# A fused decoder layer: routed weights of the experts spread by DMA, routing and small DVE steps in other rounds

## The chip, the cores and the metric

One core of a Trainium2 chip runs the whole layer as one program. The metric is the device time of one execution in microseconds (us), lower is better. The engines are PE (matrix products), ACT, DVE and POOL (elementwise work), and SP, whose queue issues most of the DMAs. They run side by side, each in its own program order, and wait for each other by semaphores.

## The reference

```python
x = x + local_attention(layernorm(x))              # 8 heads, chunks of 12 with 12 past, relative positions
x = x + cross_attention(layernorm(x), ctx_1024)    # 16 heads of 64, 512 context rows, rotary keys, clipped scores
x = x + ffn(layernorm(x))
def ffn(x):                                        # 1024 tokens of 128
    x_addr = x @ P_w.T
    dw1, dw2, dw3 = (route(x_addr @ U.T) for U in (U1, U2, U3))  # top 3 of 12, softmax over them, else 0
    h = gelu(sum_e (x @ W1[e].T) * dw1[:, e])      # 128 -> 512, 12 experts
    return sum_e (h @ W2[e].T) * dw2[:, e] + dw3 @ b2
```

Four batch entries of 256 tokens; all in fp32.

## The kernel before

The program has three stages. The local attention takes about the first 60 us. The cross attention follows in 32 **rounds** (`for r in range(NPAIR)`), each for a pair of heads of one batch entry (8 rounds per entry): PE makes the scores of the next pair (L1211), the values of a coming group (`unit`, L1027 to L1029), the rotated keys of a coming pair (`key_products`, L1016 to L1018, up to round 25), in even rounds the queries of the next four heads (`queries`, L1145 to L1147), then the weighted values (`weigh_values`, L1230) and the sums of the weights (`sum_weights`, L1240). ACT exponentiates, DVE clips (L1631), turns keys (`key_unit`, L1512 and L1517) and divides (`divide`: a reciprocal, L1638, and a product into `o_t`, L1642). POOL adds up the weights (L578, `halves_summed` L584) and adds the swapped key halves (L570). PE's `queries(j)` waits until `divide` has read the bank that it writes, `divide` of round r - 1 being DVE's first step in round r. DVE's round r starts when PE has made the sums of round r - 1.

Small steps are set into the rounds by tables. `LATENT_ROUNDS[b]` gives, for batch entry b, the rounds in which DVE takes the statistics of its tokens, normalizes them and takes statistics again, and normalizes again (`latents`, parts 0, 1, 2; L1457, L1451). `extras` gives the rounds after which PE turns those tokens or projects a batch entry's output (`project`, 16 products for two halves of 8, L1249; its sum into the tokens on DVE is L1650 or L1653). `context_lo` (L1503), `latents_lo` (L1602) and `output_bias` (L1597, in rounds 6 and 26) are further DVE steps. The **routing** of the first 512 tokens runs in seven stages two half rounds apart from `NORM_ROUND` = 22 on: weights, tokens, address, scores (r = 25), chosen (26), softmax (27), turn (28).

The third stage is the mixture of experts. `first_mixture(n)` runs for n = 0 to 23: two halves of 512 tokens by 12 experts, each 12 products of 128x512 (L1374 to L1376, four banks of three). Before it the tokens are multiplied by their routed weight (`expert_tokens` on DVE, L1681, or `pool_tokens` on POOL, L647), and split into `xeT_hi` (ACT, L853) and `xeT_lo` (POOL, L607). DVE also turns and splits an expert's weights for each n (`turn_weights` L1661, `weights_lo` L1667). The routed weights of a half, `dw`, are turned on PE (L1301) and copied by ACT to `gate_src`; SP stores them to DRAM and loads them back spread over all 128 partitions, three experts to a load (`store_gates` L474, `load_gates` L487, two buffers in `gates`). For the first three experts of each half, e < `GE`, no load is made: PE spreads their weights by a product with a selection matrix (`spread_weights`, L1278, six in all) from `dw1T`, which ACT and DVE make in two steps (L876, L1712) before ACT copies `gate_src`. SP's queue takes the gate loads in order between its loads of expert weights (`GATE_AT`), which each wait until a ring slot is free.

The last sums (`sum_weights(31)`) are issued after expert 0, the last projection (32 products, two token tiles) after expert 1; then come DVE's additions to x (L1817), the statistics of the second half's tokens and its routing (`ROUTE_2`: tokens in expert 5, address and scores in 6, chosen 7, softmax 8, turn 9). After expert 11 ACT applies the Gelu (L957) to the banks that expert 12 writes next. The second mixture follows from about 354 us on.

## Time and profile before

| | |
|---|---|
| time, median of 3 runs | 425.8 us (425.7 to 427.06) |
| the profiled execution: its time, its span | 426.81 us, 424.9 us |
| PE busy | 402.7 us, 95% of the span, 3040 instructions |
| DVE busy | 336.0 us, 79%, 655 |
| POOL busy | 257.5 us, 61%, 225 |
| ACT busy | 178.2 us, 42%, 282 |
| mean granted TensorE clock | 0.996 |

PE is busy nearly throughout, but its products are pipelined and their ends are modelled, so a short wait can hide in a busy stretch. Busy shares are means over stages of different limits: DVE is busy 19.9 of 20 us in some stretches of the rounds and half of the time in the second mixture. What an edit is worth is read from the wait that ends last at its place: the entries in brackets at a PE instruction, and the engine named there.

### The profile page before, as it was taken

The numbers are of one execution on the slowest core, as the hardware profiler recorded it, in microseconds if no ns is written. First come the engines' busy times: TensorE is split into PE (matmuls) and PEld (weight loads), VectorE is DVE, ScalarE is ACT, GpSimd is POOL, SyncE is SP. The second block draws the span as 40 slices with busy tenths as digits, with TensorE's granted clock in tenths as the row PEclk, the third lists the DMA queues.
The fourth block names the chain that finished last, engine by engine and source line by source line (L and its number), as shares of the span: only waits on it lengthen the run. The fifth ranks groups of instructions, "written<-read, shape, count | busy, mean of one in ns | idle before, by whom it ended". The sixth has DMA issues, their size and how long they took to land.

```text
span 424.9 us, 8269 instructions
## 1 busy us (share of the span) xinstructions
PE 402.7 (95%) x3040; PEld 296.0 (70%) x3040; DVE 336.0 (79%) x655; ACT 178.2 (42%) x282; POOL 257.5 (61%) x225
## 2 busy tenths in 40 slices
PE   3988799999999999999999998999999999999996
PEld 2666686667657776677766675687767788888884
DVE  8887759999989988998877997885778772655554
ACT  6867354545445245544263534336256443000000
POOL 6823549999998977998987686758335840000000
PEclk9999989999999999999999999999999999999999
DMA  7687422221211112111111162547347640000000
GB/s 181 160 214 105 89 66 61 52 81 44 51 44 32 38 37 52 26 45 43 40 37 39 41 110 65 137 69 153 54 107 155 148 64 2 6 13 8 6 6 14
DMA packets 84746, 28.63 MB, mean 67 GB/s; under 512 B 71957, under 2 KB 79050, under 8 KB 84706
## 3 DMA queue, kind: packets, MB, share of 16 engines
q1 hardware_dynamic: 81748, 26.80, 28.6%
q10 hardware_dynamic: 2958, 1.30, 1.4%
q8 instruction: 25, 0.41, 0.4%
q14 instruction: 15, 0.12, 0.1%
HBM read 17.67 MB, written 2.02 MB: 46 GB/s over the span
## 4 chain that ended last, share of the span: by engine, by line
PE 58%; DVE 31%; issue 4%; ACT 2%; DMA 2%; ACTq 1%; POOL 0%; DVEq 0%
PE psum L1230 7%; DVE rden L1638 7%; PE psum L1211 6%; DVE e_sb L1631 6%; PE psum L1414 5%; PE psum L1415 5%; PE psum L1413 5%; PE psum L1374 4%; PE psum L1376 4%; PE psum L1375 4%; PE psum L1249 3%; PE psum L1240 2%; DVE rope_b L1512 2%; DVE xn L1457 2%; DVE kT L1517 2%
## 5 line engine op out<-in xcount | busy, mean ns | idle before, releaser
L578 POOL TENSOR_TENSOR e_part<-e_sb 128x512 f32<-128x512 f32 x64 | 88.4, 1397 | 25.7 <-DVE e_sb L1631 25.7
L839 ACT ACTIVATE e_sb<-psum 128x1024 f32<-128x1024 f32 x64 | 62.3, 1023 | 81.4 <-PE psum L1211 78.5
L1631 DVE TENSOR_SCALAR e_sb<-e_sb 128x1024 f32<-128x1024 f32 x64 | 63.8, 1026 | 5.9 <-ACT e_sb L839 5.9
L1211 PE MATMUL psum<-q_t,kT 64*128 64x256 f32 x512 | 64.2, 389 | 0.0
L1230 PE MATMUL psum<-e_sb,v_sb 128*64 128x256 f32 x512 | 63.8, 386 | 0.0
L1638 DVE RECIPROCAL rden<-psum 128x256 f32<-128x256 f32 x32 | 55.9, 1747 | 9.1 <-PE psum L1240 9.1
L1840 DVE SCALAR_TENSOR_TENSOR x_sb<-psum,dw,x_sb 128x128 f32<-128x128 f32 x96 | 33.7, 351 | 37.1 <-PE psum L1415 34.5
L1211 PEld LDWEIGHTS psum<-q_t,kT 64*128 64x128 f32 x512 | 46.7, 186 | 13.9 <-issue 8.4
L1230 PEld LDWEIGHTS psum<-e_sb,v_sb 128*64 128x64 f32 x512 | 33.7, 136 | 22.3 <-issue 6.6
L607 POOL TENSOR_TENSOR xeT_lo<-xeT,xeT_hi 128x512 fp32r<-128x512 f32 x24 | 31.4, 1309 | 28.7 <-ACT xeT_hi L853 28.6
L570 POOL TENSOR_TENSOR kT<-kT,raw 128x512 f32<-128x512 f32 x32 | 44.2, 1382 | 2.7 <-DMA raw<-rope_b 1.9
L584 POOL TENSOR_TENSOR e_part<-e_part 128x512 f32<-128x512 f32 x32 | 42.1, 1317 | 2.5
L1374 PE MATMUL psum<-xeT_hi,w1T_hi 128*128 128x512 f32 x96 | 38.9, 406 | 0.8 <-ACT h_f L957 0.5
L1414 PE MATMUL psum<-w2T_lo,h_hi 128*128 128x512 f32 x96 | 38.0, 396 | 0.0
L1415 PE MATMUL psum<-w2T_hi,h_lo 128*128 128x512 f32 x96 | 37.8, 394 | 0.0
L1376 PE MATMUL psum<-xeT_hi,w1T_lo 128*128 128x512 f32 x96 | 37.5, 390 | 0.0
L1375 PE MATMUL psum<-xeT_lo,w1T_hi 128*128 128x512 f32 x96 | 37.4, 390 | 0.0
L1413 PE MATMUL psum<-w2T_hi,h_hi 128*128 128x512 f32 x96 | 37.3, 389 | 0.0
L853 ACT ACTIVATE xeT_hi<-xeT 128x512 fp32r<-128x512 f32 x24 | 15.2, 632 | 27.5 <-DVE xeT L1681 21.9
L1374 PEld LDWEIGHTS psum<-xeT_hi,w1T_hi 128*128 128x128 f32 x96 | 18.0, 188 | 7.0 <-issue 2.6
L1517 DVE TENSOR_TENSOR kT<-psum,cosT 128x512 f32<-128x512 f32 x32 | 21.7, 677 | 0.0
L1661 DVE STREAM_TRANSPOSE psum<-w_raw 128x512 f32<-128x512 f32 x24 | 17.4, 726 | 4.8 <-DMA w_raw<-in_L_ffn_W_dram 2.8
(202 smaller groups left out, 733.3 us busy)
## 6 DMA issues: line engine op xcount, KB each, us to landing
raw<-rope_b SPq DMA_DIRECT2D x116, 64.0 KB, 2.0
w_raw<-in_L_ffn_W_dram SPq DMA_DIRECT2D x96, 64.0 KB, 2.3
gates<-gate_dram SPq DMA_DIRECT2D x6, 768.0 KB, 5.0
ctx_sb<-in_ctx_dram SPq DMA_DIRECT2D x4, 256.0 KB, 6.7
vbd<-v_dram SPq DMA_DIRECT2D x16, 52.6 KB
v_dram<-v_tok SPq DMA_DIRECT2D x4, 136.0 KB
raw<-in_L_xattn_Wkv_dram SPq DMA_DIRECT2D x2, 256.0 KB, 5.5
kT<-in_L_xattn_Wkv_dram SPq DMA_DIRECT2D x2, 256.0 KB, 4.8
```

The costliest lines, as they stand in the source:

```text
L578: pool.tensor_tensor(e_part[:, p % 2, half, :, :], e_sb[:, i % ERING, :, 0, :], e_sb[:, i % ERING, :, 1, :], ALU.add)\
L839: act.activation(e_sb[:, i % ERING, :, :, :].rearrange("p a k t -> p (a k t)"), psum[:, a:a + 2, :].rearrange("p a b -> p (a b)"), ACT.Exp ...
L1211: mm = pe.matmul(psum[:, 2 * (i % 2) + a, t * S:(t + 1) * S], key_slot(p)[rows, kt * P:(kt + 1) * P], q_t[rows, j % 2, p % 2, :], start=Tr ...
L1230: mm = pe.matmul(psum[DX * a:DX * a + DX, pv_bank(p), 0:S], v_sb[g % 2][:, kt, 2 * pp + a, :], e_sb[:, i % ERING, a, t, :], start=(kt == 0 ...
L1374: pe.matmul(bank(c), w1T_hi[:, e, c, :], hi, start=(e == 0), stop=False)
L1375: pe.matmul(bank(c), w1T_hi[:, e, c, :], lo, start=False, stop=False)
L1376: mm = pe.matmul(bank(c), w1T_lo[:, e, c, :], hi, start=False, stop=(e == NE - 1))
L1413: pe.matmul(o, hi, w_hi, start=(c == 0), stop=False)
L1414: pe.matmul(o, hi, w_lo, start=False, stop=False)
L1415: mm = pe.matmul(o, lo, w_hi, start=False, stop=(c == HC - 1))
L1631: dve.tensor_scalar(e, e, E_LO, E_HI, ALU.max, ALU.min).then_inc(s["clip_done"], 1)
L1638: dve.reciprocal(rden[:, p % 2, :], psum[:, pv_bank(p), S:2 * S]).then_inc(s["rden_done"], 1)
```

## The change

All routed weights now come by DMA. `spread_weights`, `pick`, `spread` and `dw1T` are gone, with ACT's and DVE's two steps for `dw1T`. `GLOADS` has eight loads instead of six; the first (experts 0 to 2 of the first half) lands in a part of `w1T_hi` that is filled with expert weights only later. `expert_tokens` and `pool_tokens` read all gates from SBUF. The routing of the first half starts at round 20 instead of 22, that of the second half one expert earlier. The last sums are issued after half of expert 0, the last projection after half of expert 1; DVE's additions and statistics that follow stand one expert earlier. The steps for the latents, the context rests, the output bias and two projections stand in other rounds; the first statistics of an entry's latents are apart from the rest. The diff, cut (tables first, then SP, ACT, PE and DVE):

```diff
-    GLOADS = [(half, q) for half in range(2) for q in range(1, NE // GE)]
-    GATE_AT = {4: (0, 1), 10: (2,), 14: (3,), 16: (4,), 20: (5,)}
+    GLOADS = [(half, q) for half in range(2) for q in range(NE // GE)]
+    GATE_AT = {4: (0, 1, 2), 10: (3,), 13: (4,), 15: (5,), 19: (6,), 22: (7,)}
+    GATE_HOME = 6
...
-        LATENT_ROUNDS = {1: (0, 1, 2), 2: (9, 10, 11), 3: (14, 15, 16)}
+        LATENT_ROUNDS = {1: (1, 2, 3), 2: (5, 6, 10), 3: (11, 13, 16)}
+        LATENT_TURN = {4: 1, 12: 2, 18: 3}
+        CONTEXT_REST = {8: 2, 17: 3}
...
-        extras = {rounds[2] + 1: ("latents", b) for b, rounds in LATENT_ROUNDS.items()}
+        extras = {r: ("latents", b) for r, b in LATENT_TURN.items()}
...
-                extras[b * PPB + 3 + 2 * t] = ("project", b - 1, t)
+                extras[b * PPB + (1 if b == 2 else 3) + 2 * t] = ("project", b - 1, t)
...
+        def gate_tile(g, j):
+            if g:
+                return gates[:, (g - 1) % 2, j, :]
+            return w1T_hi[:, GATE_HOME + j, :, :].bitcast(F32).rearrange("p c q -> p (c q)")
...
-        NORM_ROUND = (B - 1) * PPB - 2
+        NORM_ROUND = (B - 1) * PPB - 4
-        ROUTE_2 = {"tokens": 5, "address": 6, "scores": 6, "chosen": 7, "softmax": 8, "turn": 9}
+        ROUTE_2 = {"tokens": 4, "address": 5, "scores": 5, "chosen": 6, "softmax": 7, "turn": 8}
...
                 if g == 0:
+                    sp.wait_ge(s["unit_ps"], len(UNIT))
+                    sp.wait_ge(s["misc_ps"], MISC_NO["keys", NPAIR - 1] + 1)
+                elif g == 1:
                     sp.wait_ge(s["pv_ps"], STEPS - HG)
                     sp.wait_ge(s["round_q_ps"], NQ - 1)
...
-                    act.activation(dw1T[0:NE, :], bank(at, NE), ACT.Copy).then_inc(s["dw1_hi_done"], 1)
-                    act.wait_ge(s["dw1_lo_done"], half + 1)
...
-                if r in (NPAIR - 3, NPAIR - 2):
-                    spread_weights(r - NPAIR + 3)
...
+                        if EXTRA_NO[what]:
+                            pe.wait_ge(s["extra_read"], EXTRA_NO[what])
...
-                    if c == 1 and beside == "spread":
-                        spread_weights(NE)
+                    if c == 1 and beside == "sums":
+                        sum_weights(NPAIR - 1)
+                    elif c == 1 and beside == "project":
+                        for t in range(TPB):
+                            last = project(B - 1, t, psum[:, 7, t * D:(t + 1) * D])
+                        last.then_inc(s["tail_ps"], 1)
...
-                first_mixture(n, "spread" if n + 2 == NE else ROUTE_MID.get(n))
-                if n == 0:
-                    sum_weights(NPAIR - 1)
-                if n == 1:
-                    for t in range(TPB):
-                        mm = project(B - 1, t, psum[:, 7, t * D:(t + 1) * D])
-                    mm.then_inc(s["tail_ps"], 1)
+                first_mixture(n, ("sums", "project")[n] if n < 2 else ROUTE_MID.get(n))
...
-                if e < GE:
-                    dve.wait_ge(s["spread_ps"], half * GE + e + 1)
-                    gate = bank(gate_bank(n))
-                else:
-                    gate = gates[:, g % 2, e % GE, :]
-                dve.tensor_tensor(xeT[:, n % 2, :], gate, xnT[:, half, :], ALU.mult).then_inc(s["xe_done"], 1)
+                dve.tensor_tensor(xeT[:, n % 2, :], gate_tile(g, e % GE), xnT[:, half, :], ALU.mult).then_inc(s["xe_done"], 1)
...
-            beside = {6: (output_bias, 0), NPAIR - 6: (output_bias, 1)}
+            beside = {4: (output_bias, 0), NPAIR - 6: (output_bias, 1)}
...
-                if r - 1 in CONTEXT_ROUND:
-                    context_lo(CONTEXT_ROUND[r - 1])
+                if r in CONTEXT_REST:
+                    context_lo(CONTEXT_REST[r])
...
-                if n == 4:
+                if n == 2:
                     final_norm(1, 1)
-                if n == 2:
+                if n == 1:
                     dve.wait_ge(s["tail_ps"], 1)
```

## Rows read from the trace of the kernel before

**Rows 1.** Windows: us, then busy us of PE, PEld, DVE, ACT, POOL, clock, DMA
```profile
100.00:120.00 20.00, 19.09 (x142) 13.27 (x140) 19.90 (x23) 9.86 (x14) 18.29 (x13) 1.00 0.17 43
345.00:385.00 40.00, 40.00 (x175) 32.65 (x174) 19.92 (x49) 5.97 (x11) 2.20 (x2) 1.00 0.05 10
```
**Rows 2.** Lines grouped, PE: count, busy us, mean ns, idle before
```profile
L1278 PE MATMUL psum<-dw1T,spread 44*128 44x512 f32 x6 | 3.1, 520 | 0.8 <-DVE xeT L1681 0.8
```
**Rows 3.** PE's waits in the rounds: one grouped row (total, times, longest), three from the timeline
```profile
PE psum L1145 <- DVE o_t L1642: 3.6, 5, 1.3
...
118.34 0.35 PE L1145 MATMUL psum<-lat_hi,wq_hi 128*128 128x256 f32 x1 [0.91 <-DVE o_t L1642]
144.36 0.50 PE L1016 MATMUL psum<-wkv_hi,ctx_hi 128*128 128x512 f32 x1 [0.67 <-DVE x_sb L1650]
256.43 0.35 PE L1145 MATMUL psum<-lat_hi,wq_hi 128*128 128x256 f32 x1 [1.26 <-DVE o_t L1642]
```
**Rows 4.** DVE timeline, rounds 1 to 8: start us, busy us
```profile
69.53 1.74 DVE L1638 RECIPROCAL rden<-psum 128x256 f32<-128x256 f32 x1
71.64 1.57 DVE L1457 TENSOR_SCALAR xn<-x_sb,mv,rstd 128x128 f32<-128x128 f32 x2
73.93 1.57 DVE L1631 TENSOR_SCALAR e_sb<-e_sb 128x1024 f32<-128x1024 f32 x2
...
114.28 1.79 DVE L1503 TENSOR_TENSOR ctx_lo<-ctx_f,ctx_hi 128x512 fp32r<-128x512 f32 x1
115.99 1.75 DVE L1638 RECIPROCAL rden<-psum 128x256 f32<-128x256 f32 x1
```
**Rows 5.** Timeline of DVE at rounds 25 and 28, and of PE after round 27
```profile
232.90 1.76 DVE L1638 RECIPROCAL rden<-psum 128x256 f32<-128x256 f32 x1 [1.47 <-PE psum L1240]
254.08 1.75 DVE L1638 RECIPROCAL rden<-psum 128x256 f32<-128x256 f32 x1
...
251.19 2.05 PE L1249 MATMUL psum<-wo_sb,o_t 128*128 128x128 f32 x16
```
**Rows 6.** PE timeline, from round 29 to the last projection
```profile
264.76 2.05 PE L1249 MATMUL psum<-wo_sb,o_t 128*128 128x128 f32 x16
273.81 0.47 PE L1278 MATMUL psum<-dw1T,spread 44*128 44x512 f32 x1 [0.76 <-DVE xeT L1681]
280.61 3.73 PE L1249 MATMUL psum<-wo_sb,o_t 128*128 128x128 f32 x32
```
**Rows 7.** DVE timeline, from round 29 to the last division; POOL's last sum of weights
```profile
266.85 0.29 DVE L1653 TENSOR_TENSOR x_sb<-psum,x_sb 128x128 f32<-128x128 f32 x1 [1.72 <-PE psum L1249]
279.65 0.42 DVE L1642 TENSOR_TENSOR o_t<-psum,rden 128x256 f32<-128x256 f32 x1
...
274.10 1.29 POOL L584 TENSOR_TENSOR e_part<-e_part 128x512 f32<-128x512 f32 x1
```
**Rows 8.** The tile gates: DVE's products (ns min/median/max), and the loads' time to landing
```profile
L1681 DVE TENSOR_TENSOR xeT<-gates,xnT x10: 658/684/1301, 280.0 to 345.2; 128x512 f32<-128x512 f32 x10
...
DMA to landing us min/median/max: 4.2/5.0/5.8
```
**Rows 9.** SP's queue in the timeline: expert weights 0 to 3, the second half's gates
```profile
244.25 9.44 SPq L509 DMA_DIRECT2D w_raw<-in_L_ffn_W_dram  x16
...
311.88 0.33 SPq L474 DMA_DIRECT2D gate_dram<-gate_src  x1
313.42 0.35 SPq L487 DMA_DIRECT2D gates<-gate_dram  x1
```
**Rows 10.** Second half: scores, turn, and expert 12's start on PE; first gated tokens on DVE
```profile
298.23 1.08 PE L1296 MATMUL psum<-uT,addrT 64*128 64x36 f32 x8
308.54 0.60 PE L1301 MATMUL psum<-ident,dw 128*12 128x128 f32 x4 [0.24 <-DVE dw L1735]
318.19 0.47 PE L1374 MATMUL psum<-xeT_hi,w1T_hi 128*128 128x512 f32 x1 [0.50 <-ACT h_f L957]
...
313.80 1.33 DVE L1681 TENSOR_TENSOR xeT<-psum,xnT 128x512 f32<-128x512 f32 x2
```

More of the change, by code:

```diff
@@ L247, in decoder_layer @@
         uT = sb("uT", [DADDR, NR * NE], F32, third)
-        pick = sb("pick", [SPLIT, NE], F32, third)
-        spread = sb("spread", [SPLIT, GE, P], F32R, third)
         gate_src = sb("gate_src", [NE, 4 * P], F32, third)
@@ L261, in decoder_layer @@
         dw = sb("dw", [P, 2, 4, NR, NE], F32, third)
-        dw1T = sb("dw1T", [SPLIT, 4 * P], F32R, third)
         h_lo = sb("h_lo", [P, 2, HC, 4 * P], F32R, third)
@@ L354, in swap_halves, with gate_sem, gate_landed @@
                      .then_inc(s[f"swapped{p % 2}"], 16)
-        def gate_bank(n):
-            return 5 if n < 2 else 5 - n % 2
+        def gate_tile(g, j):
+            if g:
+                return gates[:, (g - 1) % 2, j, :]
+            return w1T_hi[:, GATE_HOME + j, :, :].bitcast(F32).rearrange("p c q -> p (c q)")
+        def gate_sem(g):
+            return s["ld_gate2" if g == 0 else f"ld_gate{(g - 1) % 2}"]
+        def gate_landed(queue, g):
+            queue.wait_ge(gate_sem(g), 16 if g == 0 else 16 * ((g - 1) // 2 + 1))
         def pv_bank(p):
@@ L366, in queries_bank @@
             return pv_bank(2 * j - 1) if j else MISC_BANK
-        NORM_ROUND = (B - 1) * PPB - 2
+        NORM_ROUND = (B - 1) * PPB - 4
         ROUTE = {"weights": 2 * NORM_ROUND, "tokens": 2 * NORM_ROUND + 2, "address": 2 * NORM_ROUND + 4, "scores": 2 * NORM_ROUND + 6,
                  "chosen": 2 * NORM_ROUND + 8, "softmax": 2 * NORM_ROUND + 10, "turn": 2 * NORM_ROUND + 12}
-        ROUTE_READ = {"weights": ("rt_done", 2), "tokens": ("fT_done", 1), "address": ("addr_done", 1), "scores": ("z_done", 1)}
-        FILLED = 20
-        ROUTE_2 = {"tokens": 5, "address": 6, "scores": 6, "chosen": 7, "softmax": 8, "turn": 9}
-        ROUTE_MID = {5: "tokens", 6: "scores", 9: "turn"}
+        ROUTE_READ = {"weights": ("rt_done", 2), "tokens": ("fT_done", 1), "address": ("addr_done", 1), "scores": ("z_done", 1), "turn": ("gate_src_done", 1)}
+        FILLED = 18
+        ROUTE_2 = {"tokens": 4, "address": 5, "scores": 5, "chosen": 6, "softmax": 7, "turn": 8}
+        ROUTE_MID = {4: "tokens", 5: "scores", 8: "turn"}
         POOL_TOKENS = tuple(range(4, NE, 2)) + tuple(range(NE + 4, 2 * NE, 2))
@@ L486, in load_gates @@
                 rows = gate_dram[half, q * GE:(q + 1) * GE].rearrange("e t -> (e t)")
-                sp.dma_start(gates[:, g % 2, :, :].rearrange("p e t -> p (e t)"), rows.partition_broadcast(P)).then_inc(s[f"ld_gate{g % 2}"], 16)
+                if g:
+                    to = gates[:, (g - 1) % 2, :, :].rearrange("p e t -> p (e t)")
+                else:
+                    to = w1T_hi[:, GATE_HOME:GATE_HOME + GE, :, :].bitcast(F32).rearrange("p e c q -> p (e c q)")
+                sp.dma_start(to, rows.partition_broadcast(P)).then_inc(gate_sem(g), 16)
             for p in range(5, 8):
@@ L645, in pool_tokens @@
                 pool.wait_ge(s["xeT_lo_done"], n - 1)
-                pool.wait_ge(s[f"ld_gate{g % 2}"], 16 * (g // 2 + 1))
-                pool.tensor_tensor(xeT[:, n % 2, :], gates[:, g % 2, e % GE, :], xnT[:, half, :], ALU.mult).then_inc(s["xe_pool_done"], 1)
+                gate_landed(pool, g)
+                pool.tensor_tensor(xeT[:, n % 2, :], gate_tile(g, e % GE), xnT[:, half, :], ALU.mult).then_inc(s["xe_pool_done"], 1)
             for n in range(1, 2 * NE):
                 token_rest(n)
-                if n == 4:
+                if n == 3:
                     rstd_of(LN_F + NT // 2, NT // 2)
@@ L873, in route @@
                     act.wait_ge(s["dw1_ps"], half + 1)
-                    if half == 0:
-                        act.wait_ge(s["fill_done"], 3)
-                    act.activation(dw1T[0:NE, :], bank(at, NE), ACT.Copy).then_inc(s["dw1_hi_done"], 1)
-                    act.wait_ge(s["dw1_lo_done"], half + 1)
                     if half:
@@ L943, in _ @@
                     tokens_hi(n + 2)
-                if n == 4:
+                if n == 3:
                     final_normalize(1)
@@ L1418, in _ @@
             for n in range(2 * NE):
-                if n < 2 * NE - 2 and n + 2 != NE:
-                    spread_weights(n + 2)
                 if n in BIAS:
@@ L1709, in route @@
                     return
-                if stage == "turn":
-                    dve.wait_ge(s["dw1_hi_done"], half + 1)
-                    dve.tensor_tensor(dw1T[REST:SPLIT, :], bank(at, NE), dw1T[0:NE, :].bitcast(F32), ALU.subtract)\
-                       .then_inc(s["dw1_lo_done"], 1)
                 if stage not in ("chosen", "softmax"):
```

31 lines of the change are left out of this document (6 added, 25 removed).

## The prediction

> **What bounds the kernel now.** I read the page first (PE busy for 95% of the span), then the windows, then PE's timeline for the waits in brackets, then the timeline of whichever engine a bracket names. The windows show that the page's share hides two stages [rows 1]. From 345 us on PE has no idle time at all, 175 products in 40.0 us, 0.229 us each, with DVE half idle: there only work taken from PE counts, and the change takes none there. In the rounds, at 100 to 120 us, PE is busy for 19.1 of 20 us but DVE for 19.9: PE and DVE are level, and where DVE's round runs over, PE waits. Its waits are short: five of them before the queries, 3.6 us in all, and one of 0.67 before a value product, all on DVE [rows 3]. The third stage to read is the passage from the rounds into the experts, 260 to 320 us, where each few microseconds have another engine that comes last.
>
> The sum is made against the profiled execution, 426.81 us with a span of 424.9 (1.9 lie around it), and carried over to the median of 425.8, which lies 1.0 below that execution.
>
> **The six spread products** cost 0.52 each on PE, 3.1 us in all, with a wait of 0.76 before the third [rows 2, 6]. That is the price if PE were the last engine wherever one stood. It isn't, so each place is taken by itself below.
>
> **Latents, context rests, bias (rounds 0 to 19).** DVE runs from its division at 69.53 (round 1) to the one at 115.99 (round 8) without a wait, and PE's queries of round 8 then wait 0.91 for that division [rows 3, 4]. So what is added to DVE in rounds 1 to 7 moves PE's round 8. A normalization with its statistics takes 71.64 to 73.93 = 2.3 us, 0.7 of it statistics; a context rest 114.28 to 115.99 = 1.7 [rows 4]. Into rounds 1 to 7 come the first statistics of entry 1 (from round 0, 0.7), those of entry 2 (0.7) and its first normalization (2.3); out goes one context rest (1.7). The bias and the low half of the latents only change rounds within. That is +2.0 us for DVE. The 0.7 from round 0 frees DVE there, so +1.3 at PE's round 8. Rounds 9 to 16 lose the same steps, and the wait of 0.67 at 144.36 can go with the share of the other three query waits (3.6 less 0.91 and 1.26: 1.4) that lies there, put at a third, 0.5: 1.2 regained [rows 3]. I take +0.1. The ends: +2.0 if nothing is regained, and -3.0 if every wait but round 28's goes (3.6 less 1.26, plus 0.67). The wait that is added for PE before an extra step asks for readers of a round or more ago, and behind it stand only the next round's scores: nothing. Moving two projections from rounds 19 and 21 to 17 and 19 costs PE the same products.
>
> **Routing of the first half, two rounds earlier.** Today rounds 25 to 27 (scores, chosen, softmax) hold DVE from 232.90 to 254.08, 21.2 us; PE has made those rounds by 251.19, 18.3 us after the sums that released DVE at 232.90 [rows 5]. PE's queries of round 28 pay 1.26 for it, after a projection of 2.0 has covered part [rows 3, 5]. In rounds 23 to 25 DVE has two more key turns, two 128x512 products each at about 0.68 as the tokens' [rows 8], 1.3 each, and loses the bias of round 26 (1.7, as the context rest): 21.2 + 2.6 - 1.7 = 22.1. PE has two more sets of three key products, 0.7 each: 19.7. DVE is then 2.4 late instead of 2.9, but before round 26's queries stands a value unit of 0.7 as cover where the projection of 2.0 stood: wait 1.26 - 0.5 + 1.3 = 2.1 in place of 1.26, +0.8. The other end is -1.3, no wait at all. The chosen and softmax steps stand between POOL's additions and may run faster or slower than in the old rounds, so I take +0.2. The weights' transpose, token and address products are PE's in any round: nothing.
>
> **The gates of the first experts** come by DMA without cost as I read it. SP is busy with expert weights until 244.25 + 9.44 = 253.7; store to load takes 313.42 - 311.88 = 1.5, the landing up to 5.8: 261.0 [rows 8, 9]. DVE multiplies the first tokens right after its addition at 266.85 [rows 7]. The cover is 5 us. Were it gone, each microsecond would go onto DVE's chain below. The two loads behind it wait for round 28's queries as today's two do, and the next weight load for DVE's first transpose, so SP's queue keeps its order.
>
> **Round 29 to expert 2.** DVE waits 1.72 for the projection that PE starts at 264.76, adds it at 266.85, and from there runs without a wait to the end of the last division, 279.65 + 0.42 = 280.07 [rows 6, 7]: tokens and weights of experts 0 to 2 are in that chain, and none of it goes. The spread of round 29 stands before that projection, so the chain starts 0.5 earlier. The spread of round 30 and the one at 273.81 with its 0.76 stand beside the chain: PE only arrives earlier at what it waits for. The last sums amid expert 0 wait for POOL's addition (274.10 + 1.29 = 275.4 today, 274.9 then), with half of expert 0 queued behind; PE passes expert 1's first half at 274.9 + 0.5 + 12 x 0.229 = 278.2. The last projection needs the division: 280.07 - 0.5 = 279.55. Behind it, and this is new, stand six products of expert 1, 1.4 us. Today the projection starts at 280.61 with nothing of expert 1 left. So expert 2 starts at 279.55 + p + 1.4 against 280.61 + p, p being the projection itself: **+0.35**. Here the spreads' removal is used up.
>
> To this comes c, what the tokens of experts 0 to 2 cost more when their gate lies in SBUF. Ten such products take 0.684 in the median, as from PSUM (0.68, two in 1.33), but one took 1.30 [rows 8, 10]. I take c = 0 by the median; the other end is three slow ones, 1.9. The Trainium skill (SBUF — State Buffer, Who interferes with whom) speaks against this edit: a DVE instruction with two SBUF inputs contends with a GpSimd instruction that reads SBUF, and the one that comes second waits for the whole of the other. The one slow product agrees, and by that rule c would be above 0 here.
>
> **Experts 2 to 12.** The second half's scores stand at 298.23, the turn at 308.54 after a wait of 0.24 for DVE, 10.3 later [rows 10]. The scores come one expert (12 x 0.229 = 2.75) earlier against expert 2 (today 284.1, 280.61 + 3.5), so the turn at 284.1 + 14.1 - 2.75 + 10.3 = 305.75 in today's frame. From the turn to the store it is 3.3 us today, through ACT, DVE and ACT [rows 9, 10]; with only one ACT copy left about 0.5 + 0.9 = 1.4: 307.15. The load follows 1.5 later, and lands 4.2 to 5.8 after: 312.85 to 314.45, 313.65 with the median [rows 8, 9]. From the first gated tokens at 313.80 to expert 12 it takes 4.39, since ACT must split the tokens of 12 and 13 before it loads the Gelu's table and frees the banks [rows 10]. So expert 12 starts at 313.65 + 4.39 = 318.05 against 318.19: -0.15, from -0.95 to +0.65. The three spreads of this stretch (1.6 us of PE) vanish in that wait. DVE stands before the missing gates in the meantime, and behind it weights that the second mixture needs much later.
>
> **Sum:** +0.1 + 0.2 + 0.35 - 0.15 = +0.5, so 427.3 for the profiled execution and 426.3 for the median: within what can't be told from no change. A measurement of this kernel tells about 0.3% (1.3 us).
>
> **Rivals.** (1) *DVE's rounds don't lengthen.* The moved steps fall where DVE stands behind POOL today; then the waits of 0.91, 0.67 and 1.26 go and nothing replaces them: -2.85 + 0.35 - 0.15 = -2.65, 423.2. For it speaks that the statistics read one tensor and that a DVE round with nothing extra is well under PE's; against it the 46 us of DVE without a wait [rows 4]. (2) *The products have their full price*: PE is the last engine wherever a spread stood, so 3.1 + 0.76 go, 421.9. DVE's unbroken chain [rows 7] speaks against it. (3) *Port contention*: POOL adds weights all through 266 to 275 us, so all three tokens of c are slow; +0.5 + 1.9 = 428.2. It decides from c = 0.8 on. The skill's rule above would have it so wherever POOL starts first. (4) *Gates late*: the second half's load lands at 5.8 us with weight loads around it; expert 12 then starts 0.65 late instead of 0.15 early, and with the upper end of the routing (+0.8) it gives +0.5 + 0.8 + 0.6 = 427.7. That the DMA replaces the product without a gain is the forecast itself.
>
> **How the numbers follow.** Forecast 0.40; rival 1 0.24 and rival 2 0.08, so faster by over 0.3% 0.32; rival 3 0.18 and rival 4 0.10, so slower 0.28. The likeliest case alone has 425.1 to 427.0. Both signs hold much of the chance, so the range takes in rivals 1, 3 and 4 and the ends of the terms around them: 422.6 to 428.5; rival 2 and the ends of the first term lie outside.
>
> **What would show it.** In the trace after: PE's wait before the queries of rounds 4, 6 or 8 in place of round 2, and of round 26 in place of 28; a PE wait before the last projection of about 1.4 us, on the division; a wait of some tenths before the last sums, on POOL; L1681's first three at 0.68 or at 1.3; gates that land 4 to 6 us after their issue, and expert 12 within 1 us of them plus 4.4. The prediction is wrong if DVE shows idle time in rounds 3 to 7, if the last projection starts right behind expert 1's first half, or if expert 12 starts on the end of expert 11 alone.

## The result, and the profile after

| | before | after |
|---|---|---|
| median | 425.93 us (425.7 to 427.06, 4 runs) | 432.81 us (429.53 to 436.15, 4 runs) |
| ratio to before | | 1.012, 95% interval 1.0073 to 1.0166 |
| the profiled execution: time, span | 426.81, 424.9 us | 429.53, 427.6 us |

The change makes the kernel slower, where the forecast was no measurable change, 426.3 us in a range of 422.6 to 428.5. The profiled execution of after is its shortest, so there are two things to explain: the 2.7 us between the two profiled executions, and the 3.3 us from there to after's median. One of after's four runs, 436.15, counts as slow and is in its median but not in the ratio: without it the median is 431.91.

The page of after, first part (busy us and share of the span):

```profile
PE 400.4 (94%) x3034; PEld 293.9 (69%) x3034; DVE 339.3 (79%) x653; ACT 177.0 (41%) x280; POOL 256.0 (60%) x222
```

The six products are gone, and PE is busy 2.3 us less than before in a longer span: it waits 27.2 us in place of 22.2. The timeline of after's PE, its waits in brackets and the points at which I cut the span (L1153 are the queries, L1248 the sums of weights, L1257 the last projection, L1367 experts 12 and 16, L1410 and L1412 the second mixture):

```profile
67.06 0.60 PE L1248 MATMUL psum<-e_part,ones 128*64 128x256 f32 x4
...
90.93 0.35 PE L1153 MATMUL psum<-lat_hi,wq_hi 128*128 128x256 f32 x1 [1.24 <-DVE o_t L1631]
104.95 0.35 PE L1153 MATMUL psum<-lat_hi,wq_hi 128*128 128x256 f32 x1 [1.05 <-DVE o_t L1631]
131.05 0.36 PE L1153 MATMUL psum<-lat_hi,wq_hi 128*128 128x256 f32 x1 [0.69 <-DVE o_t L1631]
243.00 0.35 PE L1153 MATMUL psum<-lat_hi,wq_hi 128*128 128x256 f32 x1 [1.06 <-DVE o_t L1631]
...
269.06 0.60 PE L1248 MATMUL psum<-e_part,ones 128*64 128x256 f32 x4
275.24 0.65 PE L1248 MATMUL psum<-e_part,ones 128*64 128x256 f32 x4 [1.11 <-POOL e_part L599]
280.64 3.81 PE L1257 MATMUL psum<-wo_sb,o_t 128*128 128x128 f32 x32 [1.29 <-DVE o_t L1631]
308.15 0.60 PE L1294 MATMUL psum<-ident,dw 128*12 128x128 f32 x4 [1.67 <-DVE dw L1715]
319.51 0.47 PE L1367 MATMUL psum<-xeT_hi,w1T_hi 128*128 128x512 f32 x1 [1.21 <-ACT h_f L965]
336.11 0.50 PE L1367 MATMUL psum<-xeT_hi,w1T_hi 128*128 128x512 f32 x1 [0.51 <-POOL xeT_lo L622]
356.61 0.39 PE L1410 MATMUL psum<-w2T_hi,h_hi 128*128 128x512 f32 x1
...
423.57 0.40 PE L1412 MATMUL psum<-w2T_hi,h_lo 128*128 128x512 f32 x1
```

From starts such as these, each profile falls into five stretches: (a) sums of the first round to sums of round 30, (b) on to the last projection, (c) on to expert 12, (d) on to the second mixture, (e) its first to its last product. They are the table by which all kernels are compared below.

| kernel | median us (runs) | ratio to before, interval | a | b | c | d | e |
|---|---|---|---|---|---|---|---|
| before | | | 202.53 | 9.94 | 37.58 | 36.31 | 66.33 |
| after | 432.81 (4) | 1.012, 1.0073–1.0166 | 202.00 | 11.58 | 38.87 | 37.10 | 66.96 |
| x1 after again | 434.37 (4) | 1.0155, 1.0095–1.0216 | 204.89 | 11.57 | 39.05 | 38.09 | 66.96 |
| x2 late loads earlier | 430.37 (7) | 1.0092, 1.0058–1.0125 | 202.82 | 11.59 | 39.11 | 36.31 | 66.96 |
| x3 sums, projection not amid | 429.64 (10) | 1.0082, 1.0053–1.0111 | 202.09 | 11.61 | 38.65 | 37.06 | 66.97 |
| x4 rounds only | 426.72 (10) | 1.0008, 0.9981–1.0034 | 202.84 | 9.95 | 37.58 | 36.31 | 66.33 |
| x5 = x2 + x3 | 430.55 (4) | 1.0104, 1.0068–1.0141 | 202.72 | 11.60 | 38.34 | 36.31 | 66.96 |
| x6 first half by products | 430.60 (4) | 1.0119, 1.0070–1.0169 | 203.06 | 9.37 | 39.07 | 38.09 | 66.33 |
| x7 second half by products | 429.37 (4) | 1.0078, 1.0055–1.0101 | 202.57 | 11.58 | 39.69 | 36.30 | 66.32 |
| x8 = x5 + x6 | 428.34 (10) | 1.0044, 1.0024–1.0064 | 205.92 | 9.93 | 38.42 | 36.31 | 66.33 |
| x9 padded | 431.01 (4) | 1.0109, 1.0060–1.0158 | 202.85 | 11.57 | 39.10 | 36.96 | 66.33 |
| x10 softmax first | 430.43 (6) | 1.0102, 1.0070–1.0134 | 201.86 | 11.60 | 39.16 | 37.12 | 66.97 |
| x11 x4, softmax first | 425.66 (12) | 0.9983, 0.9963–1.0003 | 202.88 | 9.94 | 37.58 | 36.32 | 66.32 |
| x12 x4, softmax amid | 430.15 (6) | 1.0086, 1.0056–1.0116 | 204.93 | 9.92 | 37.58 | 36.28 | 66.33 |
| x13 x11, first half by DMA | 427.66 (12) | 1.0019, 1.0004–1.0034 | 201.43 | 11.63 | 37.68 | 36.29 | 66.33 |
| x14 x11, second half by DMA | 427.46 (12) | 1.0025, 1.0004–1.0045 | 202.66 | 9.94 | 38.30 | 36.31 | 66.33 |
| x15 x11 again | 426.50 (12) | 0.9997, 0.9978–1.0016 | 202.11 | 9.92 | 37.57 | 36.31 | 66.33 |

After against before: a -0.53, b +1.64, c +1.29, d +0.79, e +0.63, together +3.82. The spans differ by only 2.7 because the profiled execution of before lost 1.1 ahead of stretch a. That is chance: over the 17 profiles stretch a starts between 66.88 us (x12) and 69.75 (x9), where no edit is aimed. Stretch a itself spreads too, by its first four rounds above all: x11 and x15 are the same kernel and have 202.88 and 202.11. So a difference of less than about 0.8 in a says nothing. b and e repeat to some hundredths in the same code; among after, x1, x9 and x10, whose instructions there are the same, c spreads by 0.3 and d by 1.1.

The windows ahead of stretch a (clock is the 1.00 or 0.52 near the end of a row), of before:

```profile
52.60:56.10 3.50, 3.50 (x39) 2.92 (x41) 1.60 (x7) 1.92 (x5) 1.61 (x2) 0.52 0.38 94
```

and of after:

```profile
52.60:56.10 3.50, 3.09 (x77) 2.40 (x77) 1.90 (x8) 1.82 (x4) 1.45 (x2) 1.00 0.38 96
```

In before, PE did 39 products there at about the half level of its clock (1.2 GHz), where after did 77 at the full one (2.4 GHz). In six other profiles (x5, x8, x9, x11, x14, x15) the clock of 50 to 70 us is below 1.00 too, in kernels of both kinds.

### The profile page after: what moved, and what is told of

Read it like the earlier page. It is cut to its first block, busy times and chain, and to the rows that moved or that the text cites. A ratio compares the mean times of both kernels' runs of the same rounds, so it can differ in the third digit from the quotient of the medians.

```text
span 427.6 us, 8251 instructions
## 1 busy us (share of the span) xinstructions
PE 400.4 (94%) x3034; PEld 293.9 (69%) x3034; DVE 339.3 (79%) x653; ACT 177.0 (41%) x280; POOL 256.0 (60%) x222
## 4 chain that ended last, share of the span: by engine, by line
PE 54%; DVE 30%; issue 5%; SPq 4%; ACT 3%; DMA 2%; ACTq 1%; POOL 1%; DVEq 0%; POOLq 0%
PE psum L1238 7%; DVE rden L1627 7%; PE psum L1219 7%; DVE e_sb L1620 5%; PE psum L1411 5%; PE psum L1412 5%; PE psum L1410 5%; SPq L524 4%; PE psum L1257 3%; PE psum L1367 3%; PE psum L1369 2%; PE psum L1368 2%; DVE rope_b L1501 2%; DVE kT L1506 2%; DVE xn L1446 2%
## 5 line engine op out<-in xcount | busy, mean ns | idle before, releaser
L1367 PE MATMUL psum<-xeT_hi,w1T_hi 128*128 128x512 f32 x96 | 38.7, 403 | 2.0 <-ACT h_f L965 1.2
L1412 PE MATMUL psum<-w2T_hi,h_lo 128*128 128x512 f32 x96 | 37.9, 395 | 0.0
L1410 PE MATMUL psum<-w2T_hi,h_hi 128*128 128x512 f32 x96 | 37.7, 393 | 0.0
L1367 PEld LDWEIGHTS psum<-xeT_hi,w1T_hi 128*128 128x128 f32 x96 | 18.0, 188 | 8.3 <-POOL xeT_lo L622 2.4
L544 POOL TENSOR_SCALAR veps<-mv 128x4 f32<-128x4 f32 (+1 forms) x16 | 9.2, 572 | 21.8 <-DVE mv L1443 21.8
```

The costliest lines, as they stand in the source:

```text
L1367: pe.matmul(bank(c), w1T_hi[:, e, c, :], hi, start=(e == 0), stop=False)
L1410: pe.matmul(o, hi, w_hi, start=(c == 0), stop=False)
L1412: mm = pe.matmul(o, lo, w_hi, start=False, stop=(c == HC - 1))
```

## The experiments

Each ratio is to runs of before on the same chip.

**x1: the changed kernel once more.** No edit.

> The changed kernel itself, once more. Theory A (the tail: gate products from SBUF that wait for POOL, gate loads 6 and 7 that land too late; on top of it PE's clock, which falls in some executions after PE's new waits): fastest execution near 429.5, others up to 436, their mean granted clock 0.99 to 0.996, and where a profile catches it a stretch at half clock after one of PE's waits between 270 and 320 us. Rival B (the spread of the times has nothing to do with the clock, say the gate loads' landing): slow executions at a clock of 1.0 as well.

434.37 us: the loss is real. Its profile, 435.51 us, is 6.0 longer than the first one of the same program, in three places: a is 2.89 longer, d 0.99, and a starts 2.0 later. Most of the last is a wait for a load in the local attention, which after's first profile does not have:

```profile
48.07 2.52 PE L1103 MATMUL psum<-vbd,prT 96*32 96x68 f32 x128 [1.54 <-DMA vbd<-v_dram]
```

Stretch a parts in round 25. The timeline of after there: the first product of the softmax on DVE, POOL's two additions of weights that run beside it, and PE's weighted values behind its wait (1.06, above):

```profile
239.14 0.30 DVE L1709 TENSOR_TENSOR chosen<-chosen,ez 128x144 f32<-128x144 f32 x1
...
237.50 3.06 POOL L593 TENSOR_TENSOR e_part<-e_sb 128x512 f32<-128x512 f32 x2 [1.66 <-DVE e_sb L1620]
...
243.88 1.08 PE L1238 MATMUL psum<-e_sb,v_sb 128*64 128x256 f32 x8
```

The same in x1:

```profile
241.33 1.41 DVE L1709 TENSOR_TENSOR chosen<-chosen,ez 128x144 f32<-128x144 f32 x1
...
239.69 2.89 POOL L593 TENSOR_TENSOR e_part<-e_sb 128x512 f32<-128x512 f32 x2 [1.66 <-DVE e_sb L1620]
...
246.38 0.36 PE L1153 MATMUL psum<-lat_hi,wq_hi 128*128 128x256 f32 x1 [2.25 <-DVE o_t L1631]
247.73 1.98 PE L1238 MATMUL psum<-e_sb,v_sb 128*64 128x256 f32 x8
```

This is a race. One addition takes 1.27, so in x1 the second of the pair begins about 239.69 + 2.89 - 1.27 = 241.31, and DVE's product at 241.33: it takes 1.41 instead of 0.30 and ends when POOL is through, so it came second. In after the second addition begins at 239.12 or 239.13, against 239.14 for DVE; here the product is short and POOL's pair took 3.06 instead of 2.89, so DVE came first. The starts alone do not tell who won: the product's stands 0.01 to 0.02 behind the addition's in all ten profiles with this order (after, x1 to x9). It was lost in two of them, x1 and x8. The lost race makes PE wait 2.25 before round 26's queries instead of 1.06. Then its eight products take 1.98 instead of 1.08, with the granted clock at the half level. From the sums of round 25 to those of round 26 it is 10.54 us in x1 and x8, and 7.79 to 7.84 in the eight others: a lost race costs 2.7, and the rest of the 2.89 is a's spread. The window 240 to 250 us of x1 and then of after:

```profile
240.00:250.00 10.00, 7.75 (x49) 4.69 (x44) 8.96 (x12) 3.03 (x4) 8.24 (x6) 0.83 0.18 46
```

```profile
240.00:250.00 10.00, 8.94 (x66) 5.54 (x64) 8.89 (x10) 5.56 (x8) 8.90 (x7) 1.00 0.30 59
```

A mean of 0.83 over 10 us is 3.4 us at half the clock. Whether the race is the cause, or happens to go with it, is left to x10 to x12.

**x2: the second half's last two gate loads earlier.**

```diff
-    GATE_AT = {... 15: (5,), 19: (6,), 22: (7,)}
+    GATE_AT = {... 15: (5,), 17: (6,), 20: (7,)}
```

> The changed kernel, with gate loads 6 and 7 in SP's queue at expert weights 17 and 20 instead of 19 and 22. Theory A: POOL's wait of 2.9 us and DVE's of 2.2 us for gates go, with them about 0.8 us before the second mixture: 0.8 us below the changed kernel. Rival: those waits were hidden but for PE's 0.5, and nothing changes.

430.37 us, and d is 36.31, to the hundredth what it was before. In after, SP issues the load for experts 18 to 20 at 328.96 (before: 319.53), and POOL waits 2.94 for it; timeline of after:

```profile
328.96 0.57 SPq L502 DMA_DIRECT2D gates<-gate_dram  x1
...
333.53 1.29 POOL L659 TENSOR_TENSOR xeT<-gates,xnT 128x512 f32<-128x512 f32 x1 [2.94 <-DMA gates<-gate_dram]
```

In x2 it goes out at 325.37, with expert 12 at 320.84, and POOL's product has no wait:

```profile
325.37 0.57 SPq L502 DMA_DIRECT2D gates<-gate_dram  x1
...
332.01 1.75 POOL L659 TENSOR_TENSOR xeT<-gates,xnT 128x512 f32<-128x512 f32 x1
```

So the late load costs 0.8 in after's profile and 1.8 in x1's and x6's (d of 38.09). That x2's median lies 2.4 to 4.0 below those of after and x1 is more than this, though x2 has the race as they do. In its profile the race was won; how often its other executions lost it is not shown.

**x3: last sums and last projection behind whole experts again**, as in the kernel before; **x5: that and x2's edit together.**

```diff
-                first_mixture(n, ("sums", "project")[n] if n < 2 else ROUTE_MID.get(n))
+                first_mixture(n, ROUTE_MID.get(n))
+                if n == 0:
+                    sum_weights(NPAIR - 1)
+                if n == 1:
...
```

> The changed kernel, with the last sums after expert 0 and the last projection after expert 1, as before. Theory A: the projection starts when the last division is done, about 280.6, in either order, so the six products of expert 1 no longer stand behind it: expert 2 starts 1.4 us earlier, the whole 1 to 1.4 us faster, and PE's waits of 1.1 before the sums and 1.3 before the projection go, so fewer executions at a lower clock. Rival C (the order amid the experts pays, since DVE's residual comes earlier): slower by up to 1 us.

> The changed kernel with both edits: sums and projection after whole experts, and gate loads 6 and 7 at expert weights 17 and 20. Theory A (each removes waits of PE at its own place): the two gains add in an undisturbed execution, about 1 and 0.8 us off 429.5, so 427.7 to 428.3, still 1.5 to 2 above before for the gate products that wait for POOL; and the spread of the times shrinks, a median below 429. Rival: one wait takes the place of the other, and it stays at 429.6 as with the order alone.

429.64 and 430.55 us; neither came down to what was expected. b is unmoved (11.61 and 11.60): the projection waits for the division, whichever products lie ahead of it. c gets 0.2 shorter in x3, and 0.8 in x5 against x2. Six products of 0.229 behind the projection should be 1.4; the waits for dw and for the Gelu after them absorb the rest. The order is a small part of the loss.

**x4: the change's tables for the rounds alone** (latents, contexts, bias, projections, routing from round 20), everything else as before. The main lines that differ from the kernel before:

```diff
+        LATENT_ROUNDS = {1: (1, 2, 3), 2: (5, 6, 10), 3: (11, 13, 16)}
+        LATENT_TURN = {4: 1, 12: 2, 18: 3}
+        CONTEXT_REST = {8: 2, 17: 3}
+        NORM_ROUND = (B - 1) * PPB - 4
+            beside = {4: (output_bias, 0), NPAIR - 6: (output_bias, 1)}
```

> The kernel before, with only the rounds part of the change: latents, context rests, bias, two projections and the first half's routing in the new rounds; gates and tail as before. Theory A: within 0.7 us of the kernel before, 425.3 to 426.7. Rival D (the rounds are where the loss comes from): 428 or more.

426.72 us, a ratio of 1.0008 (0.9981 to 1.0034): no change that can be measured, a +0.3, which is within its spread, b to e as before. The rounds' tables are not where the median goes, unless the race is lost; x4's profile won it, and none of its ten executions was above 428.9.

**x6: the first half's first three gates by products again; x7: the second half's; x8: x6 with the orders of x5.** `pick`, `spread`, `dw1T` and their steps come back for the half named: `BY_PRODUCT` is (0,) in x6 and x8 and (1,) in x7.

```diff
+    BY_PRODUCT = (0,)
+    GLOADS = [... if q or half not in BY_PRODUCT]
+                if e < GE and half in BY_PRODUCT:
+                    dve.wait_ge(s["spread_ps"], BY_PRODUCT.index(half) * GE + e + 1)
+                    gate = bank(gate_bank(n))
```

> The changed kernel, with the gates of the first half's experts 0 to 2 spread by products again (no load for them, two steps for dw1T back, three products on PE); all else as changed. Theory A (port): DVE's first three gate products go from 1.54, 1.59 and 0.86 us to 0.68 each, 1.8 less in DVE's chain up to the last division, against 0.5 more ahead of it for the first product: the last projection starts 1.3 us earlier, and the fastest execution is near 428.2. Rival E (the chain is long for another reason, such as the clock or the landing of the loads): no gain or a loss of 0.5 to 1.5 for the three products.

> The changed kernel, with the gates of the second half's experts 0 to 2 spread by products again, and the gate loads of that half at expert weights 14, 16 and 20 as in the kernel before. Theory A: expert 12 starts as late as in the changed kernel (the load's landing and the products' steps take the same), within 0.5 us; the late loads' waits go, 0.8 us: fastest near 428.7 with a smaller spread. Rival F (the landing of the second half's first load is what costs): expert 12 starts 1 us or more earlier.

> All three edits on the changed kernel: first half's gates of experts 0 to 2 by products, sums and projection after whole experts, gate loads 6 and 7 earlier. What is left of the change is the rounds and the second half's gates by DMA. Theory A: the loss is gone, 425.5 to 427. If it stays above 428, something else in the change costs time.

x6: b falls from 11.58 to 9.37. The tokens of experts 0 to 2 explain it. DVE and POOL in after's timeline:

```profile
265.67 1.54 DVE L1665 TENSOR_TENSOR xeT<-w1T_hi,xnT 128x512 f32<-128x512 f32 x1
272.48 1.59 DVE L1665 TENSOR_TENSOR xeT<-w1T_hi,xnT 128x512 f32<-128x512 f32 x1
276.11 0.86 DVE L1665 TENSOR_TENSOR xeT<-w1T_hi,xnT 128x512 f32<-128x512 f32 x1
280.07 0.42 DVE L1631 TENSOR_TENSOR o_t<-psum,rden 128x256 f32<-128x256 f32 x1
...
265.39 1.27 POOL L599 TENSOR_TENSOR e_part<-e_part 128x512 f32<-128x512 f32 x1
270.62 2.90 POOL L593 TENSOR_TENSOR e_part<-e_sb 128x512 f32<-128x512 f32 x2 [1.38 <-DVE e_sb L1620]
275.15 1.27 POOL L622 TENSOR_TENSOR xeT_lo<-xeT,xeT_hi 128x512 fp32r<-128x512 f32 x1
```

and DVE in x6's, where the gate lies in PSUM:

```profile
266.51 0.68 DVE L1710 TENSOR_TENSOR xeT<-psum,xnT 128x512 f32<-128x512 f32 x1
272.46 0.67 DVE L1710 TENSOR_TENSOR xeT<-psum,xnT 128x512 f32<-128x512 f32 x1
275.16 0.68 DVE L1710 TENSOR_TENSOR xeT<-psum,xnT 128x512 f32<-128x512 f32 x1
```

Each of after's three ends 0.55 us after the POOL instruction that had begun ahead of it (267.21 after 266.66, 274.07 after 273.52, 276.97 after 276.42), so the greater part of its work is done once POOL is through. x6's three also begin while POOL is at work (its instructions from 266.02, 270.60 and 274.80), and with the gate in PSUM none is longer for it. That is 1.54 + 1.59 + 0.86 - 2.03 = 1.96 on a chain without slack. The Trainium skill (SBUF — State Buffer, Who interferes with whom) says that a DVE instruction with two inputs from SBUF contends with a GpSimd instruction that reads SBUF, and that whichever is issued first holds the shared ports for its whole length; these rows agree, with these numbers.

x6's whole time does not show the gain: its fastest execution is 429.61, where 428.2 was expected. In its profile e is 0.63 shorter and b 2.2, but d is 0.99 longer, by the late load, and a 1.06: 0.44 of that are the spreads of rounds 29 and 30, the rest a's spread. From the sums of round 24 to the last projection, past the rounds in which a spreads, it is 46.18 against after's 47.95, 1.77 less: the 1.96 without one spread of 0.22.

x7: d is back at 36.30 and e at 66.32, but c is 39.69: three spreads of 0.52 come on top of the wait for dw, since the routing stays one expert early, and the wait before expert 12 takes up only part (0.35 there, 1.21 in after). x8 has the least of what changed and is the fastest of the three by its median, 428.34, still above the 428 that its expectation named as the bound for something else at work; its profile lost the race in round 25 (that product took 1.42, the wait was 2.23), which is why its a is 205.92.

**x9: three unused tiles where `pick`, `spread` and `dw1T` lay.** No instruction differs from after's, only addresses.

```diff
+        pad_a = sb("pad_a", [44, NE], F32, third)
+        pad_b = sb("pad_b", [44, GE, P], F32, third)
         gate_src = sb("gate_src", [NE, 4 * P], F32, third)
...
+        pad_c = sb("pad_c", [44, 4 * P], F32, third)
         h_lo = sb("h_lo", [P, 2, HC, 4 * P], F32R, third)
```

> The changed kernel with three unused tiles of the sizes of pick, spread and dw1T at their old places, so that h_lo lies where it lay before; no instruction differs. Theory: the second mixture is longer in the changed kernel (66.96 us from its first to its last product, 66.33 before) because of where its operands lie: here 66.3, and the rest as in the changed kernel, so 0.6 us less in all. Rival: the instruction stream does it (fewer products ahead, other loads): 66.96 stays.

e is 66.33 again. The second mixture's products, grouped by line between 360 and 420 us (count, busy us, mean ns), of after:

```profile
L1411 PE MATMUL psum<-w2T_lo,h_hi 128*128 128x512 f32 x87 | 34.6, 397 | 0.0
L1412 PE MATMUL psum<-w2T_hi,h_lo 128*128 128x512 f32 x86 | 34.0, 395 | 0.0
L1410 PE MATMUL psum<-w2T_hi,h_hi 128*128 128x512 f32 x86 | 33.8, 393 | 0.0
```

and of x9:

```profile
L1414 PE MATMUL psum<-w2T_lo,h_hi 128*128 128x512 f32 x86 | 34.1, 396 | 0.0
L1415 PE MATMUL psum<-w2T_hi,h_lo 128*128 128x512 f32 x86 | 33.9, 394 | 0.0
L1413 PE MATMUL psum<-w2T_hi,h_hi 128*128 128x512 f32 x87 | 33.8, 389 | 0.0
```

The product next behind the one that reads `h_lo` takes 393 ns instead of 389, and the others 1 more. So 0.63 us of the loss is nothing but where tiles lie once three are gone; all kernels here with those tiles, or of their size, show 66.33. Which of the moved tiles it is, and why, wasn't tried. The whole time (431.01) spreads too far to show 0.6.

**x10 to x12: the race by itself.** The first half's softmax moves within DVE's round 25: right behind the division, where POOL is idle (x10 in after, x11 in x4), or between clips and key turn, where POOL's first addition runs (x12, in x4). The edit of x10 and x11, and that of x12, which puts the same two lines lower:

```diff
                 if stage == "softmax":
-                    route_softmax(half)
+                    if half:
+                        route_softmax(half)
...
             for r in range(NPAIR):
                 if r:
                     divide(r - 1)
+                if 2 * r == ROUTE["softmax"]:
+                    route_softmax(0)
```

```diff
...
                     clip(2 * r + 3)
+                if 2 * r == ROUTE["softmax"]:
+                    route_softmax(0)
                 if r + K_LEAD < NPAIR:
```

> The changed kernel with the first half's softmax (four DVE steps, 1.3 us) in round 25 right behind the division, where POOL has no addition running, instead of behind the key turn. Theory of the race: in the changed kernel the first of these steps (two inputs from SBUF) meets POOL's two additions and takes 0.30 or 1.41 us depending on which comes first; where it loses, PE waits 2.25 before round 26's queries and then runs 3.4 us at half the clock, about 3.8 us in all. Then here the step takes 0.30 each time, the wait is 1.1 or less, and the median falls to 430.0 to 431.0 with few runs above 432. Rival: the slow executions come from the late gate loads or from elsewhere: median stays at 432.5 to 434.5.

> Before plus the change's tables for the rounds (which alone gave 426.72 us), with the first half's softmax right behind the division of round 25. Theory of the race: product of 0.30 each time, wait before round 26's queries 1.1 or less, median 425.3 to 426.3 and none above 428. Rival: the clips and with them POOL's additions start 1.3 us later and the sums of weights follow, so PE waits there instead: 426.7 to 427.5.

> Before plus the change's tables for the rounds (426.72 us), with the first half's softmax between the clips and the key turn of round 25, where POOL's first addition is running. Theory of the race: the first product always comes second and takes 0.9 to 1.4 us, the wait before round 26's queries is 2.0 to 2.4, the clock's half level follows for 3.4 us, and the median is 428.5 to 430. Rival: the wait grows but the clock stays at its full level: 427.5 to 428. Second rival: the cost is in neither: 426.7.

430.43, 425.66 and 430.15 us. x11 and x12 have the same instructions on all engines, and four of DVE's in another place part their medians by 4.5 us. The timeline of x11:

```profile
238.68 0.30 DVE L1734 TENSOR_TENSOR chosen<-chosen,ez 128x144 f32<-128x144 f32 x1
...
244.59 0.35 PE L1147 MATMUL psum<-lat_hi,wq_hi 128*128 128x256 f32 x1 [0.70 <-DVE o_t L1646]
```

and of x12, with its window behind it:

```profile
237.58 1.38 DVE L1734 TENSOR_TENSOR chosen<-chosen,ez 128x144 f32<-128x144 f32 x1
...
243.73 0.36 PE L1147 MATMUL psum<-lat_hi,wq_hi 128*128 128x256 f32 x1 [2.14 <-DVE o_t L1646]
```

```profile
240.00:250.00 10.00, 7.86 (x49) 4.34 (x47) 7.80 (x10) 4.07 (x6) 8.26 (x7) 0.83 0.31 60
```

The product of 1.38, the wait of 2.14 and the clock at 0.83 come together here by the edit, as by chance in x1 and x8. From the sums of round 25 to those of round 26 it is 10.49 us in x12 and 7.45 in x11: 3.0 of the 4.5 are shown in the traces. The rest is not: x12's profiled execution is its fastest, 427.76, and what its longer ones lost besides was not traced. In x10 the race is out of after: its median is 430.43, and 4 of 6 executions lie below 430.8, but one took 433.43, so not every long execution is a lost race.

**x13 to x15: each half's gates by DMA alone, on x11.** x13 has the first half's three by DMA (products for the second, all orders as before); x14 the second half's, with its routing one expert early and x2's loads; x15 is x11 again.

> Before with the change's tables for the rounds and the softmax behind the division (425.66 us), and the first half's first three experts' gates by DMA; the second half's by products, its routing and the last sums and projection where they stood before. Theory of the port: the three tokens take some 1.5, 1.6 and 0.9 us instead of 0.68, the last projection starts 1.2 us later from the first round's sums than before even though the spreads are gone: 426.6 to 427.2. Rival, the prediction's own step (tokens at 0.68, a spread less ahead of the chain): 425.2 to 425.7.

> The same base, with the second half's first three experts' gates by DMA, its routing one expert earlier and the third and fourth gate loads of that half in experts 17 and 20; the first half's by products. Theory: the routing one expert earlier makes PE wait 1.65 us for dw before the turn, and the gates still come last at expert 12 (wait of 1.4), against three spreads of 0.52: 0.8 us later from the last projection to expert 12, 426.3 to 426.8. Rival, the prediction's own step (0.15 us earlier): 425.4 to 425.8.

> Before with the change's tables for the rounds and the first half's softmax behind the division of round 25, as the base of the two others: 425.3 to 426.1, so 0.997 to 0.999 of the kernel before. Rival: the lower median of the earlier run was chance, and it comes out at the kernel before's own median.

427.66, 427.46 and 426.50 us. By these medians the first half's DMA costs 1.16 and the second's 0.96; the intervals of the ratios overlap, so the sizes rest on the stretches. x15 came out above its range, and its rival holds: x11's lower median was chance. x13 and x14, whose ranges were set from x11's 425.66, lie above theirs by 0.5 and 0.7. In x13 the three tokens take 1.57, 1.59 and 0.89, as in after, with nothing else of the passage changed, and b is 1.7 longer; in rounds 28 to 30, where the two spreads stood, a is 0.44 shorter. In x14, c is 0.73 longer; its PE timeline at the turn and at expert 12:

```profile
308.86 0.60 PE L1328 MATMUL psum<-ident,dw 128*12 128x128 f32 x4 [1.66 <-DVE dw L1771]
320.38 0.47 PE L1403 MATMUL psum<-xeT_hi,w1T_hi 128*128 128x512 f32 x1 [1.37 <-ACT h_f L984]
```

The routing one expert early meets POOL there. Two softmax products of after (timeline of DVE and POOL):

```profile
305.35 0.86 DVE L1709 TENSOR_TENSOR chosen<-chosen,ez 128x144 f32<-128x144 f32 x1
306.84 1.25 DVE L1715 TENSOR_TENSOR dw<-chosen,zsum 128x144 f32<-128x144 f32 x1
...
304.75 1.29 POOL L622 TENSOR_TENSOR xeT_lo<-xeT,xeT_hi 128x512 fp32r<-128x512 f32 x1 [1.59 <-ACT xeT_hi L865]
306.67 1.26 POOL L622 TENSOR_TENSOR xeT_lo<-xeT,xeT_hi 128x512 fp32r<-128x512 f32 x1 [0.62 <-ACT xeT_hi L865]
```

Before, they took 0.28 at 307.26 and 0.31 at 308.18, with POOL idle. So 1.5 us of what the earlier routing gains goes on the same ports. A product of the stage ahead of them (into `chosen`, from `zr` and `z`) went the other way: 0.99 in before at 304.93, behind POOL's instruction from 304.46, and 0.31 in after. What is lost in all is 0.8.

The parts add up: x15's 426.50 + 1.16 + 0.96 + 0.63 (addresses) + 0.79 (late loads) = 430.0, and x10, the changed kernel without the race, has 430.43. What lifts after's median 2.4 us above x10's, and x1's 3.9, is only in part shown. A lost race costs 2.7, but x2, x3 and x9 have the race too, with medians of 430.37, 429.64 and 431.01, and it was lost in two of ten profiles. x1's profile lost about as much again elsewhere: 2.0 ahead of stretch a and 1.0 more by the late load. Why after and x1 drew more long executions than x2, x3 and x9 stays open. No version beats before: x11 came out 0.17% below it and x15, the same kernel, 0.03%, both with intervals across 1.

## Why the prediction was wrong

The reading of **what bounds the kernel** held: PE and DVE level in the rounds, DVE's chain in the passage, PE alone at the end. So did the shape of most steps, but four sizes did not. The step that failed most plainly is the price of the first experts' tokens, c, taken as 0: it was 1.96.

**Latents, context rests, bias** (+0.1): right, as far as stretch a's spread lets it be told. The waits moved to rounds 4, 6 and 10 (1.24, 1.05, 0.69), and x4 is level with before.

**Routing in the rounds** (+0.2, from -1.3 to +0.8): right in after's profile (its wait is 1.06, against 1.26 in [rows 3]), and too small wherever the race is lost. The softmax product was already slow in before, in round 27:

```profile
251.49 1.38 DVE L1729 TENSOR_TENSOR chosen<-chosen,ez 128x144 f32<-128x144 f32 x1
```

POOL's addition had begun at 251.05. So the prediction's 21.2 us of DVE, and its wait of 2.1, hold the slow product: where the race is lost the wait is 2.14 to 2.25, as summed, and where it is won 1.1 less. The prediction took neither, but a value between. What it left out is the clock: one product that comes second costs 1.1 on DVE and 1.2 of PE's wait, and the half level behind it brings that to 2.7. Rows of before with a clock below 1.00 were there to be read, and none was in the argument.

**Gates of the first experts** at no cost: right for the landing. SP loads them at 256.58, and DVE's first tokens at 265.67 wait for nothing.

**Round 29 to expert 2** (+0.35): the structure was right, with PE waiting 1.11 for POOL before the last sums, 1.29 for the division before the projection, and six products behind it. The failed term is **c, taken as 0** with 1.9 as its other end: 1.96. The median of [rows 8] was the wrong number to take from that group: taken one by one in the timeline of before, its ten products are seven of 0.66 to 0.69 and three of 0.96, 1.28 and 1.30, and the three are those that began with a POOL instruction under way. The last of them:

```profile
345.15 1.30 DVE L1681 TENSOR_TENSOR xeT<-gates,xnT 128x512 f32<-128x512 f32 x1
...
344.61 1.29 POOL L607 TENSOR_TENSOR xeT_lo<-xeT,xeT_hi 128x512 fp32r<-128x512 f32 x1 [1.52 <-ACT xeT_hi L853]
```

It ended 0.55 after POOL (346.45 after 345.90), as after's three did. There the tokens of the first experts begin amid POOL's additions, and that was to be read before: [rows 7] has one of them. Stretches a and b were to fall by 0.76 and rose by 1.11, a miss of 1.87. Rival 3 is what happened, at its own price of 1.9; its total of 428.2 was still too low.

**Experts 2 to 12** (-0.15): right in sum. From the last projection's 280.64 to 319.51 it is 38.87, where the prediction's numbers give 38.85 (projection and six products 4.9, then 33.95). Two errors met in it: the turn waited 1.67 for dw, and turn to store, 1.25, and the landing, 4.1, were shorter than taken. The latter also shows rival 4 at this place was not the case.

**Two terms were missing.** The last two gate loads of the second half moved from experts 16 and 20 to 19 and 22 in the diff's first lines, and the prediction priced the queue's order for the first half only: +0.79. Nothing in the trace of before could show that taking three tiles away would lengthen the second mixture by 0.63, but "the change takes none there" was said as if addresses were free.

With these three, 1.87 + 0.79 + 0.63 = 3.3; less the 1.1 that before's profile had lost at half clock and after's did not, it is 2.2, the distance of the forecast for the profiled execution (427.3) from 429.53. That it fits to a tenth is in part luck, since stretch a alone spreads by 0.8. The distance of the median is explained only as far as x10: the race adds 2.7 to an execution that loses it, and how many of after's did is not shown. Rivals 1 and 2 fell: the waits in the rounds moved but did not go, and the spreads did not bring their full price. From the sums of round 28 to those of round 30, where two of them stood, it is 10.90 us in before and 10.45 in after: 0.22 each, where the prediction took 0.52, the time of one product by itself, on an engine that overlaps them.

## What to carry to other kernels

Before moving an operand of a DVE product from PSUM to SBUF, or a two-input DVE step to another place, lay POOL's timeline beside it: here a step of 0.3 us beside an addition of 1.3 cost up to 1.1 more, and a median over products that ran without POOL says nothing of it. A change that lets two engines arrive within hundredths of a microsecond can make the time itself uncertain, so time it often and move one of the two well away. Before giving a difference between two profiles to an edit, compare the stretches that the edit does not touch. Where a DMA replaces a product, price every later load whose place moves with it, not the first one alone.

## What the hardware showed that was not expected

- A PE wait of 2.14 to 2.25 us amid the rounds was followed by 3.4 us at half the clock in all three profiles that had one (x1, x8, x12: 0.83 over 240 to 250 us); behind waits of 1.06 there (after, x4) it stayed at 1.00. In x1 the wait had grown by 1.2 and the round by 2.7.
- A DVE product with both inputs in SBUF did not get through beside a POOL instruction that reads SBUF: tokens of 0.68 became 1.54, 1.59 and 0.86 and ended 0.55 after POOL's end each time. With one input in PSUM they took 0.67 and 0.68 beside POOL.
- The second mixture's products changed with the addresses of the tiles alone, 66.96 to 66.33 us.
